# Attention scores of a GNN transformer layer: two query tiles in two row groups of TensorE instead of one tile in 96 rows

## The reference

```python
q = split_heads(x @ wq + bq); k = split_heads(x @ wk + bk); v = split_heads(x @ wv + bv)
scores = einsum('bhqd,bhkd->bhqk', q, k) * 48 ** -0.5 + adj[:, None]
attn = softmax(scores, axis=-1)
ctx = einsum('bhij,bhjd->bhid', attn, v)          # back to b, n, d
x1 = rmsnorm(x + ctx @ wo + bo, alpha1, gamma1)
x2 = rmsnorm(x1 + silu(x1 @ w1 + b1) @ w2 + b2, alpha2, gamma2)   # 1536 wide
out = layernorm(x + x2)
```

## Time and profile before

| | us |
|---|---|
| median of 3 runs (1987.14 to 1990.58) | 1987.84 |
| the profiled execution's own time | 1988.0 |
| its span | 1986.0 |
| PE busy | 1931.9 (97%) |
| weight loads busy | 1703.9 (86%) |
| DVE busy | 1334.3 (67%) |
| ACT busy | 1173.4 (59%) |
| POOL busy | 675.2 (34%) |

### The profile page before, as it was taken

One profiled execution on the slowest core, in us unless ns is written; L12 is line 12 of the kernel. 1 busy time (PEld: TensorE's weight loads), 2 busy tenths in 40 slices (PEclk: granted clock), 3 DMA queues, 4 the chain that ended last, 5 costly groups with the idle time before them and its releaser, 6 DMA issues. The chain is left out here.

```text
span 1986.0 us, 35712 instructions
## 1 busy us (share of the span) xinstructions
PE 1931.9 (97%) x10336; PEld 1703.9 (86%) x10336; DVE 1334.3 (67%) x2270; ACT 1173.4 (59%) x1896; POOL 675.2 (34%) x796
## 2 busy tenths in 40 slices
PE   7999999999999999999966999999999999999998
PEld 5888888888888888888855999999999999999997
DVE  5777777777777777777756656565666555656644
ACT  4877778777787777877745433444443344444432
POOL 2000000000000000000015667766667666566643
PEclk9999999999999999999987999999999999999999
DMA  7655565555655556455633311222221122222011
GB/s 228 146 142 151 154 181 132 142 150 155 181 130 143 149 155 183 126 145 149 158 114 106 110 60 58 81 84 84 84 83 50 44 77 84 84 84 84 18 39 40
DMA packets 107363, 226.86 MB, mean 114 GB/s; under 512 B 15041, under 2 KB 43457, under 8 KB 105281
## 3 DMA queue, kind: packets, MB, share of 16 engines
q1 hardware_dynamic: 107328, 226.43, 39.4%
HBM read 108.93 MB, written 41.94 MB: 76 GB/s over the span
## 5 line engine op out<-in xcount | busy, mean ns | idle before, releaser
L540 DVE TENSOR_TENSOR pT_lo<-ps_t,pT_hi 128x1024 fp32r<-128x1024 f32 x256 | 313.6, 1225 | 143.9 <-ACT pT_hi L449 143.9
L449 ACT ACTIVATE pT_hi<-ps_t 128x1024 fp32r<-128x1024 f32 x256 | 262.6, 1026 | 179.0 <-PE ps_t L655 177.6
L379 POOL TENSOR_TENSOR xT_lo<-xT_raw,xT_hi 128x512 fp32r<-128x512 f32 x48 | 62.3, 1300 | 853.0 <-ACT xT_hi L428 853.0
L442 ACT ACTIVATE probs<-probs,neg_max 128x512 f32<-128x512 f32 x512 | 338.9, 712 | 5.1 <-DVE neg_max L532 5.1
L532 DVE CUSTOM_DVE_ANT_0 probs<-ps_s,adj_s 128x512 f32<-128x512 f32 x448 | 291.0, 687 | 39.7 <-PE ps_s L646 32.6
L1129 DVE TENSOR_TENSOR h_lo<-hidden,h_hi 128x512 fp32r<-128x512 f32 x192 | 169.0, 881 | 169.6 <-ACT h_hi L1033 169.6
L655 PEld LDWEIGHTS ps_t<-ident,probs 128*128 128x128 f32 x2048 | 241.1, 141 | 35.7 <-issue 1.6
L655 PE MATMUL ps_t<-ident,probs 128*128 128x128 f32 x2048 | 267.2, 273 | 1.0 <-DVE pT_lo L540 1.0
L1249 PE MATMUL ps_y<-w_hi,h_hi 128*128 128x384 f32 x768 | 257.9, 336 | 0.0
L1249 PE MATMUL ps_y<-w_hi,h_lo 128*128 128x384 f32 x768 | 256.7, 334 | 0.0
L1249 PE MATMUL ps_y<-w_lo,h_hi 128*128 128x384 f32 x768 | 256.6, 334 | 0.0
(11 more groups left out here) (100 smaller groups left out, 3755.9 us busy)
## 6 DMA issues: line engine op xcount, KB each, us to landing
q_both<-stage_q SPq DMA_DIRECT2D x192, 192.0 KB, 3.9
ctx_dram<-ctx_stage SPq DMA_DIRECT2D x128, 224.0 KB
ctx_raw<-ctx_dram SPq DMA_DIRECT2D x16, 1792.0 KB, 7.2
k_hl<-stage_k SPq DMA_DIRECT2D x192, 96.0 KB, 3.2
adj_first<-in_adj SPq DMA_DIRECT2D x32, 512.0 KB, 9.3
adj_s<-in_adj SPq DMA_DIRECT2D x32, 512.0 KB, 6.0
xT_raw<-in_xT SPq DMA_DIRECT2D x16, 768.0 KB, 7.3
x<-in_x SPq DMA_DIRECT2D x16, 768.0 KB, 6.2
```

The costliest lines, as they stand in the source:

```text
L442: nc.scalar.activation(probs[:, at, :], probs[:, at, :], ACT.Exp, scale=-1.0, bias=neg_max[:, at:at + 1]).then_inc(exp_done, 1)
L449: nc.scalar.activation(pT_hi[:, h % 2, 2 * pair:2 * pair + 2, :, :], ps_t[pair][:, :, :].rearrange("p q (k i) -> p q k i", k=TT), ACT.Copy)\
L540: nc.vector.tensor_tensor(pT_lo[:, h % 2, s, :, :].rearrange("p q k i -> p (q k i)"), ps_t[pair][:, :, :].rearrange("p q n -> p (q n)"), p ...
```

## The change

The two query tiles of a pair are now tile `pair` and tile `pair + 2`, one of each half of the tokens. The first half's q lies in rows 0 to 47 and the second half's in rows 64 to 111 of a new tile `q_tiles` (high and low part beside each other, 256 tokens each); k, high and low part side by side, lies in both places of `k_hl`. Each tile of scores is three products over 48 rows (high x high, high x low, low x high), one tile from rows 0 to 47, the other from rows 64 to 111, issued alternately into the two banks. The pair waits once, for both banks of the pair before. The second copy of q_hi and its semaphore count go. adj is loaded, and pT_hi and pT_lo are written, in the order of the new pairs.

```diff
-PARTS_HI = {"q": (0, 2), "k": (0,)}
+HALF = N // 2
+GROUPS = (0, LO)
...
-        stage = {"q": sb("stage_q", [P, 3, N], FP32R), "k": sb("stage_k", [P, 2, N], FP32R)}
-        q_both = sb("q_both", [2 * DH, H, 2, N], FP32R)
-        k_hl = sb("k_hl", [2 * DH, H, N], FP32R)
+        stage = {"q": sb("stage_q", [P, 2, N], FP32R), "k": sb("stage_k", [P, 2, N], FP32R)}
+        q_tiles = sb("q_tiles", [LO + DH, H, 2, HALF], FP32R)
+        k_hl = sb("k_hl", [LO + DH, H, 2, N], FP32R)
...
             def load_adj(tile, b, pair, loaded):
-                rows = adj[b, 2 * pair * P:2 * (pair + 1) * P, :]
-                sp.dma_start(tile, rows.rearrange("(t p) k -> p t k", p=P)).then_inc(loaded, DMA)
+                rows = adj[b].rearrange("(half t p) k -> t p half k", half=2, p=P)[pair]
+                sp.dma_start(tile, rows).then_inc(loaded, DMA)
...
-                sp.wait_ge(proj_hi, proj_hi_no(b, kind, t, len(PARTS_HI[kind])))
...
-                        for part, row in enumerate((dst, DH + dst)):
+                        for half, row in enumerate(GROUPS):
                             if kind == "q":
-                                to = q_both[row:row + n, h, :, :]
-                                part_of = stage[kind][src:src + n, part:part + 2, :]
+                                to = q_tiles[row + dst:row + dst + n, h, :, :]
+                                part_of = stage[kind][src:src + n, :, half * HALF:(half + 1) * HALF]
                             else:
-                                to, part_of = k_hl[row:row + n, h, :], stage[kind][src:src + n, part, :]
+                                to = k_hl[row + dst:row + dst + n, h, :, :]
+                                part_of = stage[kind][src:src + n, :, :]
...
-                if kind == "q":
-                    act.wait_ge(proj_hi, proj_hi_no(b, kind, t, 1))
-                    nc.scalar.activation(stage[kind][:, 2, :], stage[kind][:, 0, :].bitcast(FP32), ACT.Copy)\
-                      .then_inc(proj_hi, 1)
...
-                nc.scalar.activation(pT_hi[:, h % 2, 2 * pair:2 * pair + 2, :, :],
+                nc.scalar.activation(pT_hi[:, h % 2, pair::2, :, :],
...
-                s = slice(2 * pair, 2 * pair + 2)
-                nc.vector.tensor_tensor(pT_lo[:, h % 2, s, :, :].rearrange("p q k i -> p (q k i)"),
-                                        ps_t[pair][:, :, :].rearrange("p q n -> p (q n)"),
-                                        pT_hi[:, h % 2, s, :, :].rearrange("p q k i -> p (q k i)").bitcast(FP32),
+                nc.vector.tensor_tensor(pT_lo[:, h % 2, pair::2, :, :].rearrange("p q k i -> p q (k i)"),
+                                        ps_t[pair][:, :, :],
+                                        pT_hi[:, h % 2, pair::2, :, :].rearrange("p q k i -> p q (k i)")
+                                        .bitcast(FP32),
...
-            def scores(b, h, qt):
-                if qt == 0:
+            def scores(b, h, pair):
+                if pair == 0:
...
-                wait_past(pe, logits_ready, score_no(b, h, qt) - 2)
-                toks = slice(qt * P, (qt + 1) * P)
-                nc.tensor.matmul(ps_s[qt % 2][:, :], lhsT=q_both[:, h, 0, toks], rhs=k_hl[:, h, :],
-                                 start=True, stop=False)
-                nc.tensor.matmul(ps_s[qt % 2][:, :], lhsT=q_both[:, h, 1, toks], rhs=k_hl[:, h, :],
-                                 start=False, stop=True).then_inc(scores_ready, 1)
+                wait_past(pe, logits_ready, score_no(b, h, 2 * pair + 1) - 2)
+                toks = slice(pair * P, (pair + 1) * P)
+                for n, (q_part, k_part) in enumerate(((0, 0), (0, 1), (1, 0))):
+                    for half, row in enumerate(GROUPS):
+                        last = nc.tensor.matmul(ps_s[half][:, :], lhsT=q_tiles[row:row + DH, h, q_part, toks],
+                                                rhs=k_hl[row:row + DH, h, k_part, :], start=(n == 0), stop=(n == 2))
+                        if n == 2:
+                            last.then_inc(scores_ready, 1)
```

More of the change, by code:

```diff
@@ L269, in proj_no @@
             return 2 * KT * b + proj_at(kind, t) + 1
-        def proj_hi_no(b, kind, t, parts):
-            return 3 * KT * b + sum(len(PARTS_HI[s[0]]) for s in PROJECTIONS[:proj_at(kind, t)]) + parts
         def context_at(b, p):
@@ L505, in project_lo @@
             def project_lo(b, kind, t, bank):
-                dve.wait_ge(proj_hi, proj_hi_no(b, kind, t, 1))
+                dve.wait_ge(proj_hi, proj_no(b, kind, t))
                 bias = bq_c if kind == "q" else bk_c
@@ L674, in batch @@
                     for of, h, pair in pairs_of(b, p + AHEAD):
-                        scores(of, h, 2 * pair)
-                        scores(of, h, 2 * pair + 1)
+                        scores(of, h, pair)
                     transpose_probs(b, p // 2, p % 2)
@@ L714, in _ @@
             for p in range(AHEAD):
-                for qt in range(2 * (p % 2), 2 * (p % 2) + 2):
-                    scores(0, p // 2, qt)
+                scores(0, p // 2, p % 2)
             prologue_project(len(PROLOGUE_USES) - 1)
```

## The result

The kernel after takes 2029.14 us (median; 2028.21 to 2029.4), beside 1987.49 for before on the same chip: a ratio of 1.0206, 95% interval 1.0188 to 1.0224, so 42 us slower. Forecast was 1973, and 2055 or more for a switch that empties the array.

The account below looks back on a forecast made before the run. PE, busy in 97% of the span, was taken as the bound, with room on DVE and ACT. Scores -31 and the later wait +16, all else 0, gave -15 on 1988: 1973 us, range 1943 to 2062.

Parts of the forecast that it names:

- Faster: Sign of the whole change: the run ends below 1984 us; chance 0.46.
- slower: Sign of the whole change: the run ends above 1992 us; chance 0.42.
- The switch between row groups and the full array: On PE, twice per pair, 512 times: taken as 0; upper end 0.27 us each, +138 us; 0.03 uses up the gain.
- Scores: PE's products per pair: six of 48 rows take 0.80 us instead of 0.92, -31 us over 256 pairs.
- one load ahead: Rule for PE's weight loads in scores: A and B start 0.11 us apart, 0.80 per pair; chance 0.31 with switches under 0.02.
- rival 1: PE's scores: full overlap of both row groups, free switches, 0.69 us per pair, 1947 us; chance 0.16.
- rival 2: Ahead of A1 and first transpose: switch empties the array, 2055 to 2111 us (0.23); small cost 1988 to 2009 (0.15).
- The tail: Within rival 2, at each switch: 0.16 us if the array must run empty, 2055 us with the tail alone.
- The joint wait: Next pair's scores wait for both banks: 0.8 us at p = 4 and in the last batch, 20 times, +16 us.
- the 1.68 that I took: At p = 4, when PE would reach the next scores: 0.80 + 0.80 + 0.08 us, against their start at 2.46.
- ACT, pT_hi and pT_lo, DMA: Dropped q copy (1.9 us per batch on ACT), strided pT writes, changed load sizes and order: each worth 0 on PE.
- Transposes bound by their loads: PE's eight transposes, 0.80 us: 128-column loads follow at 0.11 us, and one that follows a transpose can't be hidden.

Follow-up runs that it names:

- run 10: The kernel before, with its products of scores over rows 0 to 71 instead of 0 to 95; 1987.88 us, ratio 1.000.
- run 1: The kernel before, with its four products of scores per pair read from rows 0 to 47 alone, one group; 2078.44 us, ratio 1.0453.
- run 2: The kernel after, with both tiles of a pair read from rows 0 to 47, so six products in one row group; 2202.59 us.
- run 4: The kernel before, with its scores waiting for both banks of the pair before, nothing else changed; 1997.45 us, ratio 1.0048.
- o1: The kernel after, with the eight transposes of an iteration ahead of its scores; 2041.63 us.
- run 11: The kernel after, with ACT's copy of q's high part put back, read by nobody; 2027.86 us, ratio 1.0204.
- run 12: The kernel after, with its transposes also in the two row groups (64 rows each) and their waits ahead of the scores; 1953.61 us, ratio 0.983.
- run 13: The kernel before, scores over 96 rows kept, with the transposes in two row groups as in run 12; 1978.78 us, ratio 0.9958.
- run 14: Run 12's kernel, with head 0's context moved from iteration 3 to 4, v's tiles spread, xT's parts at 3, 4 and 5; 2028.81 us.

## Why the prediction was wrong

The measured 2029 lies inside the whole range of 1943 to 2062, but that range was wide, and none of the cases set out gives this time. Faster had 0.46 and slower 0.42.

The step that failed is *The switch between row groups and the full array*, which I took at 0. It costs 0.34 us per pair in the kernel after (0.09 + 0.11 in, 0.09 + 0.05 out), 0.17 per switch, 87 us in all. I gave ends that hold it, 0 and 0.27, named 0.03 as the point from which it decides, and then took the value of the nearest rows. But those rows were changes between 96 and 128 rows, which are no change of mode: run 10 shows that even 72 rows aren't, and run 1 that 48 are. "Nearest" was nearest in number, not in kind.

The Trainium skill had the rule: "TensorEngine Tiling (Array Packing)", section Key Properties, says that a change of tiling mode drains TensorE. The traces agree, with 0.09 us at each of the two places. The bare weight load behind it costs as much again on the way in. The prediction named this rule, and still took 0.

Point by point:

- *Scores.* Forecast one load ahead, 0.80 us per pair; measured full overlap, the 0.69 of rival 1. Run 2 confirms it. The Trainium skill's "TensorE: Matmul & The Clock Gate", Part 3, on loads for another row group, was the better guide: here such loads even start together (447.05 and 447.39, "x2"). That the three steps still take 0.34 + 0.23 + 0.23 = 0.80 us is chance: the 0.11 in it is the bare load of the way in, not a load between the groups.
- *Rivals.* What happened is rival 1 and rival 2 at once: 1947 + 512 x 0.17 = 2034. I had set them up as separate cases, each added to other terms.
- *The tail.* I took the 0.16 us by which drawn matmuls overlap as the price of emptying. It is 0.09.
- *The joint wait.* +16 forecast; +9.6 in PE's waits of after, +10 in run 4, and at p = 4 as described: DVE ended its second max at 443.13 + 0.08 and the scores started at 443.27. The place and sign were right, and so was the restart 2.46 us behind the scores before (443.27 - 440.81); the size was 1.6 times too large, because PE itself comes later than the 1.68 that I took. By the traces it needs 0.89 us for the scores and the way out, 0.81 from the first transpose to the last and 0.20 for the way in (o1), 1.90 in all.

```profile
440.81 0.96 PE L640 MATMUL ps_s<-k_hl,q_tiles 48*128 48x512 f32 x6
...
441.70 1.09 PE L651 MATMUL ps_t<-ident,probs 128*128 128x128 f32 x8
...
441.90 0.69 DVE L526 CUSTOM_DVE_ANT_0 probs<-ps_s,adj_s 128x512 f32<-128x512 f32 x1 [0.53 <-PE ps_s L640]
...
443.13 0.08 DVE L526 DVE_READ_ACCUMULATOR2_ANT neg_max<- 128x1 f32 x1
443.27 0.53 PEld L640 LDWEIGHTS ps_s<-k_hl,q_tiles 48*128 48x128 f32 x6 [0.71 <-DVE neg_max L526]
443.27 0.96 PE L640 MATMUL ps_s<-k_hl,q_tiles 48*128 48x512 f32 x6 [0.48 <-DVE neg_max L526]
```

- *ACT, pT_hi and pT_lo, DMA* at nothing: right. ACT's busy time fell by 30 us with no gain, and putting it back cost nothing (run 11). The strided pT_hi takes 1026 ns and pT_lo 1223, as before. PE waited 0.6 us, once, for the larger k.
- *Transposes bound by their loads* was a wrong reading. In after, the second load starts 0.06 us behind the bare first one (447.94, 448.00) and the block is only 0.05 longer, so such a load takes about 0.06 and doesn't bound the step of 0.109. That the 128 moving columns do is likely but not shown: with 64 of them in each group the step is 0.062 (run 12). It did no harm to this forecast, but it hid the better change.

## What to carry over

Before a product is cut to half of the rows to share the array (48 and 64 rows here), count how often the stream goes in and out: each way in or out cost about three quarters of the step of one 512-column product (0.17 against 0.23 us), so one saved product per visit doesn't pay, and neighbouring work should be brought into the mode first. Where the trace has no row of the new kind, don't take the value of rows that only look near: ask whether they cross the same border, and when two rivals can both be true, add them. A wait that joins two banks cost only where an iteration is short, and about half of it could be moved away. Where the moving of work makes PE wait, look at the granted clock behind the wait too.

## What the runs showed of the hardware

- Two row groups load weights and run at the same time, within 0.01 us of each other, for fp32r products of 48 rows (after) and fp32 transposes of 64 (run 12). Taking both tiles from one group cost 173 us (run 2).
- Going between 48 rows and the full array leaves 0.09 us empty, in both directions, behind products of 512 columns and behind transposes alike, and the next weights are not loaded ahead: 0.11 us more for a product, about 0.05 for a transpose (after, runs 1 and o1; with transposes of 64 rows in run 13). 72 and 96 rows cost nothing (run 10, before). From products of 48 rows to transposes of 64 in the same groups nothing is paid (0.23 us, run 12).
- A transpose of a 128 x 128 block of float32 takes 0.109 us in the full array; as two halves of 64 rows side by side, each into its own bank, 0.062 us (run 12).
- Behind 2.83 us in which TensorE was idle the granted clock stood at 0.50 for 6.8 us, and products of 512 columns stepped at 0.43 instead of 0.23 us (run 14).
